# Cross-attention's key and value weights split during self-attention and kept in DRAM, and the passage between the two attentions put in another order

## What is computed

```python
x = _layernorm(tgt, ln1_g, ln1_b)
q, k, v = (_heads(t) for t in jnp.split(x @ sa_wqkv, 3, axis=-1))
wei = softmax(where(causal & ~mask, q @ k.T * scale, -inf))
result = tgt + _merge(wei @ v) @ sa_wproj + sa_bproj
xq = _layernorm(result, ln2_g, ln2_b)
xs = _layernorm(src, ln2_g, ln2_b)            # context: 750 tokens
k2, v2 = (_heads(t) for t in jnp.split(xs @ ed_wkv, 2, axis=-1))
q2 = _heads(xq @ ed_wq)
result = result + _merge(softmax(q2 @ k2.T * scale) @ v2) @ ed_wproj + ed_bproj
h = relu(_layernorm(tgt, ln3_g, ln3_b) @ ff_w1 + ff_b1)
return result + (h @ ff_w2 + ff_b2)
```

## Time and profile before

| | |
|---|---|
| median of 3 runs | 1370.09 us (1369.25 to 1372.01) |
| profiled execution, first to last instruction | 1372.2 us |
| TensorE busy | 1310.9 us, 96% |
| VectorE, GpSimd, ScalarE busy | 794.4, 701.5, 662.1 us |

### The profile page before, as it was taken

How to read it: one execution, slowest core, us unless ns; L and a number is a source line. 1 busy time by engine, 2 the same in 40 slices (tenths; PEclk the granted TensorE clock), 3 DMA queues, 4 the chain that set the end, 5 groups by cost and what they waited for, 6 DMA issues and landing times.

```text
span 1372.2 us, 24578 instructions
## 1 busy us (share of the span) xinstructions
PE 1310.9 (96%) x9193; PEld 1082.5 (79%) x9193; DVE 794.4 (58%) x2007; ACT 662.1 (48%) x1609; POOL 701.5 (51%) x577
## 2 busy tenths in 40 slices
PE   7999999999899999998788999999999999999997
PEld 6888888888788888887677787878877787887874
DVE  6613223232777777776655575756757566575565
ACT  5311111232666665666433656474665647456444
POOL 3232221322444555556733767666676766667661
PEclk9999999999999999999599999999999999999999
DMA  7400102114647776547267685777677587766641
GB/s 237 145 18 16 62 31 77 46 60 117 139 86 178 166 186 148 122 123 185 63 142 119 100 128 98 132 123 125 101 127 120 101 137 104 142 101 112 90 71 41
DMA packets 100400, 151.67 MB, mean 111 GB/s; under 512 B 10197, under 2 KB 63229, under 8 KB 99514
## 3 DMA queue, kind: packets, MB, share of 16 engines
q1 hardware_dynamic: 100282, 150.11, 53.8%
HBM read 66.74 MB, written 24.12 MB: 66 GB/s over the span
## 4 chain that ended last, share of the span: by engine, by line
PE 76%; POOL 8%; issue 5%; DVE 5%; DMA 3%; ACT 2%; SPq 1%; POOLq 0%; ACTq 0%; DVEq 0%
PE ps L1727 18%; PE ps L453 11%; PE ps L164 10%; PE ps L423 10%; PE ps_pair L1744 6%; PE ps L1759 5%; PE ps L1773 5%; PE ps L1832 3%; POOL ca_partial L1586 2%; DMA ca_k_stack<-ca_keys 2%; POOL ca_xT L1473 1%; DMA sa_K_stack<-sa_rows 1%; PE ps L1207 1%; PE ps L1791 1%; PE ps L1227 1%
## 5 line engine op out<-in xcount | busy, mean ns | idle before, releaser
L1664 DVE TENSOR_REDUCE ca_maxes<-ps 112x1 f32<-112x375 f32 x512 | 256.5, 541 | 106.0 <-PE ps L1759 103.9
L1607 ACT ACTIVATE ca_probT<-ps_pair 125x448 f32<-125x448 f32 x384 | 210.3, 554 | 181.5 <-PE ps_pair L1744 179.6
L1586 POOL TENSOR_TENSOR ca_partial<-ca_partial,ca_probT 125x896 f32<-125x896 f32 x118 | 249.2, 2112 | 93.6 <-ACT ca_probT L1607 89.0
L312 POOL TENSOR_TENSOR ff_hT<-ff_hrelu,ff_hT 128x512 fp32r<-128x512 f32 (+1 forms) x64 | 77.9, 1218 | 203.2 <-DVE ff_hT L394 203.2
L1759 PE MATMUL ps<-ca_k_stack,ca_q_stack 96*112 96x376 f32 x512 | 168.7, 352 | 6.9 <-issue 3.6
L1744 PEld LDWEIGHTS ps_pair<-ca_q_stack,ca_k_stack 98*125 98x125 f32 x768 | 130.2, 186 | 44.0 <-issue 31.9
L1744 PE MATMUL ps_pair<-ca_q_stack,ca_k_stack 98*125 98x224 f32 x768 | 156.2, 285 | 1.3 <-ACT ca_probT L1607 1.2
L423 PE MATMUL ps<-ff_w,ff_hT 128*128 128x512 f32 x672 | 155.5, 390 | 0.0
L1727 PE MATMUL ps<-w_b,ca_xT 128*125 128x512 f32 x576 | 151.2, 398 | 3.1 <-POOL ca_xT L1473 2.5
L1727 PE MATMUL ps<-ca_xT,w_a 128*128 128x376 f32 x768 | 153.1, 335 | 0.0
L423 PEld LDWEIGHTS ps<-ff_w,ff_hT 128*128 128x128 f32 x672 | 125.6, 188 | 25.8
(11 more groups left out here) (145 smaller groups left out, 2433.0 us busy)
## 6 DMA issues: line engine op xcount, KB each, us to landing
ca_k_stack<-ca_keys SPq DMA_DIRECT2D x96, 376.0 KB, 8.0
sa_Q_stack<-sa_rows SPq DMA_DIRECT2D x96, 112.0 KB, 3.5
sa_K_stack<-sa_rows SPq DMA_DIRECT2D x96, 112.0 KB, 3.7
ca_q_stack<-q_out SPq DMA_DIRECT2D x96, 112.0 KB, 9.5
ctx_tokens<-in_ctx_dram SPq DMA_DIRECT2D x14, 672.0 KB
ctx_tokens<-in_L_xattn_ff_w_dram SPq DMA_DIRECT2D x16, 512.0 KB, 4.4
q_out<-sa_yT SPq DMA_DIRECT2D x16, 448.0 KB, 3.7
wp_lo<-wp_out SPq DMA_DIRECT2D x6, 1024.0 KB, 4.8
```

Source lines behind the costliest of these rows:

```text
L312: pool.tensor_tensor(hT[:, LO, m % RING, 0:width(g)], hrelu[i % 2][:, 0:width(g)], hT[:, HI, m % RING, 0:width(g)].bitcast(F32), ALU.subtr ...
L1586: pool.tensor_tensor(total, total, half(a), ALU.add).then_inc(partial_done, 1)
L1607: act.activation(probT[u // GH][0:JT, u % GH].rearrange("p a t -> p (a t)"), ps_p[u % 2][0:JT, 0:2 * T], ACT.Exp).then_inc(exp_done, 1)
L1664: dve.tensor_reduce(maxes[:, q, j, a:a + 1], ps_s[n % 3][0:TQ, 0:JH], AX_X, ALU.max).then_inc(s_read, 1)
```

## The change

- Six units instead of two are split during batches 0 to 5 (PREPARED_WEIGHTS): the two of `ed_wproj`, two of the key half and two of the value half of `ed_wkv`. Each is loaded, rounded on ScalarE, subtracted on VectorE, and both halves go to DRAM. The key half's are written in the order of w_a's columns, which takes one more ScalarE copy for each low half (`turn_prepared`).
- In slots -17 and -16 SP loads w_a and w_b, four DMAs of 1 MB. `round_next` and `keep_next` are gone.
- The first context is loaded, measured and normalised one batch earlier: statistics in batch 6, normalises in slots 11, 13, 15 of batch 6 and 1, 3, 5 of batch 7.
- T and K of group 0 move up into slots -11 to -1; V of batch 0 to slots 5 to 8; the scores of group 0, so far in cross-attention's own slots, to slots 7 to 15; K of group 1 to slot 11. `T_rest` of the first context is on GpSimd, as it is for the others.
- The memset of ones into `k_stack` becomes an item of its own, `stack_ones`, in slot 2; some waits change with it. The statistics of context 1 go to cross-attention's own slots.

The diff, without context lines and plumbing:

```diff
@@ -581,9 +582,10 @@
-NEXT_CONTEXT = [(-2, 6), (-1, 4), (-1, 5)]
-NEXT_MEASURED = {1: (0,), 2: (1,), 7: (2,), 9: (3,), 10: (4, 5)}
-NEXT_NORMALISED = {12: (0, 1), 13: (2,), 14: (3,), 15: (4, 5)}
+NEXT_CONTEXT = [(-2, 6), (-3, 10), (-3, 11)]
+NEXT_MEASURED = {0: (2,), 1: (3,), 2: (4,), 3: (5,), 9: (0,), 10: (1,)}
+LAST_MEASURED = 1
+NEXT_NORMALISED = {11: (0,), 13: (1,), 15: (2,), 17: (3,), 19: (4,), 21: (5,)}
...
@@ -609,28 +611,32 @@
-    (-10, BEHIND): [("pad",)],
-    (-2, BEHIND): [turned(0, 0)],
-    (-1, BEFORE): [turned_rest(0, 0)],
-    (-1, BEHIND): [turned(1, 0)],
-    (0, BEFORE): [turned_rest(1, 0)],
-    (0, BEHIND): [turned(2, 0)],
-    (1, BEFORE): [turned_rest(2, 0)],
-    (1, BEHIND): [turned(3, 0)],
-    (2, BEFORE): [turned_rest(3, 0), ("context", 1, 0)],
-    (2, BEHIND): [turned(0, 1)],
-    (3, BEFORE): [turned_rest(0, 1), turned(1, 1), ("K", 0, 0, 0)],
-    (4, BEFORE): [turned_rest(1, 1), ("K", 0, 0, 1), turned(2, 1)],
-    (4, BEHIND): [("K_rest", 0, 0), turned_rest(2, 1)],
-    (5, BEHIND): [turned(3, 1), ("context", 1, 1)],
-    (6, BEFORE): [turned_rest(3, 1), ("queries", 0), *values_of(0)],
-    (7, BEFORE): keys_of(0, 1),
-    (9, BEHIND): [("K_rest", 0, 1)],
-    (11, BEHIND): values_of(1),
-    (13, BEHIND): [("statistics", 1, 0), ("statistics", 1, 1)],
-    (14, BEHIND): [("statistics", 1, 2), ("statistics", 1, 3)],
-    (15, BEHIND): [*keys_of(1, 0), ("statistics", 1, 4), ("statistics", 1, 5), ("K_rest", 1, 0), *keys_of(1, 1), ("K_rest", 1, 1),
-                   ("queries", 1), ("ones",), ("weights",)],
+    (-12, BEHIND): [("pad",)],
+    (-11, BEFORE): [turned(0, 0)],
+    (-10, BEFORE): [turned_rest(0, 0), turned(1, 0)],
+    (-9, BEFORE): [turned_rest(1, 0), turned(2, 0)],
+    (-8, BEFORE): [turned_rest(2, 0), turned(3, 0)],
+    (-7, BEFORE): [turned_rest(3, 0), turned(0, 1)],
+    (-6, BEFORE): [turned_rest(0, 1), turned(1, 1)],
+    (-6, BEHIND): [("K", 0, 0, 0)],
+    (-5, BEFORE): [turned_rest(1, 1), turned(2, 1), ("context", 1, 0)],
+    (-5, BEHIND): [("K", 0, 0, 1)],
+    (-4, BEFORE): [("K_rest", 0, 0), turned_rest(2, 1), turned(3, 1)],
+    (-3, BEFORE): [turned_rest(3, 1), ("context", 1, 1)],
+    (-2, BEFORE): keys_of(0, 1),
+    (-1, BEHIND): [("K_rest", 0, 1)],
+    (2, BEHIND): [("stack_ones",)],
+    (5, BEHIND): values_of(0),
+    (6, BEHIND): [("queries", 0), *values_of(1)],
+    (7, BEHIND): [*scores_of(0, 2), ("V", 0, 2, 0)],
+    (8, BEHIND): [*scores_of(2, 4), ("V", 0, 2, 1)],
+    (11, BEFORE): [*scores_of(4, 6), *keys_of(1, 0), ("K_rest", 1, 0)],
+    (11, BEHIND): keys_of(1, 1),
+    (12, BEFORE): [("K_rest", 1, 1), ("queries", 1), *scores_of(6, 8)],
+    (13, BEFORE): scores_of(8, 10),
+    (14, BEFORE): scores_of(10, 12),
+    (14, BEHIND): scores_of(12, 14),
+    (15, BEHIND): [*scores_of(14, 16), ("ones",), ("weights",)],
...
@@ -648,7 +654,7 @@
-    return items + [("ca",) + o for o in other[start:] if o not in early]
+    return items + [("ca",) + o for o in other if o not in early]
...
@@ -675,10 +681,11 @@
-LAST_FILLS = {0: [("Y", -2, 1)], 1: [("Y", -2, 2)], 2: [("Y", -2, 3)], 4: [("P", -1, 0)], 5: [("P", -1, 1)],
-              10: [("R", -1, 0), ("R", -1, 1)], 12: [("Y", -1, 0)], 13: [("Y", -1, 1)], 14: [("Y", -1, 2), ("Y", -1, 3)]}
+LAST_FILLS = {1: [("Y", -2, 1)], 2: [("Y", -2, 2)], 3: [("Y", -2, 3)], 4: [("P", -1, 0)], 5: [("P", -1, 1)],
+              10: [("R", -1, 0), ("R", -1, 1)], 12: [("Y", -1, 0)], 13: [("Y", -1, 1), ("Y", -1, 2)], 14: [("Y", -1, 3)]}
...
-OUTPUT_WEIGHTS = [28, 44]
+PREPARED_WEIGHTS = [12, 24, 36, 48, 60, 72]
+BY_HEADS = (2, 3)
...
@@ -699,9 +706,9 @@
-    NEXT_STATISTICS = {16 * (B - 1) + i: t for i, t in NEXT_MEASURED.items()}
-    NEXT_NORMALISE = {16 * (B - 1) + i: t for i, t in NEXT_NORMALISED.items()}
-    NEXT_WEIGHTS = [16 * (B - 1) + i for i in (-1, 0, 3, 4)]
+    NEXT_STATISTICS = {16 * (B - 2) + i: t for i, t in NEXT_MEASURED.items()}
+    NEXT_NORMALISE = {16 * (B - 2) + i: t for i, t in NEXT_NORMALISED.items()}
+    NEXT_WEIGHTS = [16 * (B - 1) + i for i in (-1, 0)]
...
@@ -759,22 +766,20 @@
-        for h in range(2):
-            if n == OUTPUT_WEIGHTS[h]:
-                items.append(("load_output", h))
-            if n == OUTPUT_WEIGHTS[h] + 8:
-                items.append(("round_output", h))
-                rests[n + 1].append(("keep_output", h))
-        if n == OUTPUT_WEIGHTS[1] + 16:
-            items.append(("stage_next",))
+        for u, first in enumerate(PREPARED_WEIGHTS):
+            if n == first:
+                items.append(("load_prepared", u))
+            if n == first + 5:
+                items.append(("round_prepared", u))
+                rests[n + 1].append(("keep_prepared", u))
+            if n == first + 9 and u in BY_HEADS:
+                items.append(("turn_prepared", u))
...
-            u = NEXT_WEIGHTS.index(n)
-            items.append(("round_next", u))
-            rests[n + 1].append(("keep_next", u))
+            items.append(("load_next", NEXT_WEIGHTS.index(n)))
...
@@ -848,11 +853,13 @@
-    ws_next = WeightSplitter(weight_halves(ed_wkv[:, 0:C], w["q"], HD) + weight_halves(ed_wkv[:, C:2 * C], w["k"]),
-                             next_stage, [sem(f"wn_landed{i}") for i in range(2)], sem("wn_hi"), sem("wn_lo"))
...
-    wo_landed, wo_hi, wo_lo, wo_stored = sem("wo_landed"), sem("wo_hi"), sem("wo_lo"), sem("wo_stored")
+    wo_landed, wo_hi, wo_lo, wo_turned, wo_stored = (sem(n) for n in ("wo_landed", "wo_hi", "wo_lo", "wo_turned", "wo_stored"))
+    next_landed = [sem(f"next_landed{i}") for i in range(2)]
+    prepared = [(source.rearrange("(k p) n -> p k n", p=P)[:, 2 * h:2 * h + 2], split[:, :, 2 * h:2 * h + 2])
+                for source, split in ((ed_wproj, wp_out), (ed_wkv[:, 0:C], kv_out[0]), (ed_wkv[:, C:2 * C], kv_out[1]))
+                for h in range(2)]
...
@@ -865,6 +872,12 @@
+    def halved(u, tile):
+        return by_heads(tile) if u in BY_HEADS else tile
+
+    def interleaved(u, tile):
+        return tile.rearrange("p k (g d j) -> p (k g) j d", g=4, d=HD) if u in BY_HEADS else tile
+
...
@@ -914,22 +927,29 @@
             ws.load(sp)
-        if name == "load_output":
-            h = item[1]
-            if h == 0:
+        if name == "load_prepared":
+            u = item[1]
+            if u == 0:
                 sp.wait_ge(ws.lo_done, 2)
             else:
-                sp.wait_ge(wo_stored, 32)
-            sp.dma_start(wo_tile, ed_wproj.rearrange("(k p) n -> p k n", p=P)[:, 2 * h:2 * h + 2]).then_inc(wo_landed, 16)
-        if name == "keep_output":
-            h = item[1]
-            sp.wait_ge(wo_hi, h + 1)
-            sp.dma_start(wp_out[HI, :, 2 * h:2 * h + 2], wo_rounded).then_inc(wo_stored, 16)
-            sp.wait_ge(wo_lo, h + 1)
-            sp.dma_start(wp_out[LO, :, 2 * h:2 * h + 2], wo_tile).then_inc(wo_stored, 16)
-        if name == "stage_next":
-            sp.wait_ge(wo_stored, 64)
-            ws_next.load(sp, 0, 2)
+                sp.wait_ge(wo_stored, 32 * u)
+            sp.dma_start(wo_tile, prepared[u][0]).then_inc(wo_landed, 16)
+        if name == "keep_prepared":
+            u = item[1]
+            sp.wait_ge(wo_hi, u + 1)
+            sp.dma_start(prepared[u][1][HI], wo_rounded).then_inc(wo_stored, 16)
+            if u not in BY_HEADS:
+                sp.wait_ge(wo_lo, u + 1)
+                sp.dma_start(prepared[u][1][LO], wo_tile).then_inc(wo_stored, 16)
+        if name == "turn_prepared":
+            u = item[1]
+            sp.wait_ge(wo_turned, BY_HEADS.index(u) + 1)
+            sp.dma_start(prepared[u][1][LO], wo_rounded).then_inc(wo_stored, 16)
+        if name == "load_next":
+            i = item[1]
+            wait_psum(sp, ("QK"[i], B - 1, KT - 1))
+            for half in (HI, LO):
+                sp.dma_start(w["qk"[i]][:, half].bitcast(F32), kv_out[i, half]).then_inc(next_landed[i], 16)
         if name == "load_columns":
...
@@ -967,14 +987,12 @@
                     .then_inc(y_stored, 16)
-        if name == "keep_next" and item[1] < 2:
-            ws_next.load(sp, item[1] + 2, item[1] + 3)
         if name == "next_context":
...
             else:
-                sp.wait_ge(ws_next.lo_done, part + 2)
+                sp.wait_ge(wo_stored, 32 * len(prepared))
             first = ctx_in[0].rearrange("(p t) c -> p t c", t=CTX_TILES)
...
@@ -1015,9 +1033,7 @@
             ln2.inverse_root(pool, item[1])
-        if name == "keep_next":
-            ws_next.keep_lo(pool, item[1])
-        if name == "next_statistics" and item[1] == CTX_TILES - 1:
+        if name == "next_statistics" and item[1] == LAST_MEASURED:
             ctx_ln.inverse_root(pool, 0)
...
@@ -1051,16 +1067,17 @@
             ws.round_hi(act, item[1])
-        if name == "round_output":
-            h = item[1]
-            act.wait_ge(wo_landed, 16 * (h + 1))
-            if h == 0:
+        if name == "round_prepared":
+            u = item[1]
+            act.wait_ge(wo_landed, 16 * (u + 1))
```

(53 more changed lines are left out.)

7 lines of the change are left out of this document (5 added, 2 removed).

## The result

The changed kernel is slower: 1374.8 us in the median of 17 runs (1373.5 to 1376.5) against 1370.7 of the kernel before (17 runs, 1369.3 to 1373.7). The ratio is 1.0027 with a 95% interval of 1.0021 to 1.0034. The forecast was 1357.4 with a range of 1347 to 1369, so the time lies outside it, and on the other side of the old time.

What follows compares the result with a forecast made beforehand. TensorE's own work bounds the kernel outside the passage from self- to cross-attention, where 31 us are waiting or half clock. Terms 0.5 + 3.2 - 1.9 + 0 - 14.5 = -12.7 us, off 1370.1: 1357.4, range 1347 to 1369.

Steps and rivals of the forecast that it cites:

- The six units: Batches 0 to 5: six prepared weight units instead of two cost 0.5 us, 4 us at worst.
- Stage 640.1 to 667.5: Output product 0 to query product 0 of batch 6: no change from 27.4 us, bounded below by 23.
- Y 0 of batch 6 to score 0 of group 1: The 63.5 us from 667.5 to 731.0 fall to 49, 14.5 less, with a new 4.8 wait at group 0's first score.
- Splitting ed_wkv leaves the last batch: Stage 622.4 to 640.1 shrinks by 1.9 us, as the 2.06 wait for a weight load goes; bounds 1.2 and 2.1.
- Batch 6: First context's inverse root and normalise 0 on GpSimd ahead of a split delay the query product by 3.2 us; bounds 0, 8.1.
- From 731 on the order is as before, so nothing is given back: From the first score of cross-attention's group 1 to the end: no change, 0 us.
- signs of being wrong: Clock of 0.50 for more than 10 us; no wait at score 0; a batch 6 longer by over 5.
- signs of being right: No weight-load wait; batch 5's query product 3 us later; longest wait at score 0; last, group 1's first score 12 earlier.
- VectorE is held by GpSimd: Rival: six normalises on GpSimd beside self-attention's copies hold VectorE, half of 13.2 us landing, 6.6: 1364 us; chance 0.10.
- The clock stays down: Rival: clock stays at 0.50 from thin slots -8 to -6 past score 0, +21 us, 1378 us; chance 0.12.

Runs made afterwards that it cites:

- the second profile of before: The kernel before, with nothing changed, profiled once more: a span of 1371.8 us and a time of 1373.9 us.
- all mends together: Changed kernel with units 1 and 2 moved, memset at slot 4, query stack 1 early, normalises and low halves on VectorE, bias addition later: 1359.8 us, 0.9909.

## Why the prediction was wrong

*The six units* failed as a step. It said that such a unit lies beside products, 0.5 us in all and 4 at worst. Its price came from a batch whose unit has one cast and no second. It counted casts, subtractions and transfers as work and did not follow the new wait: the second cast needs a store to have landed, and the store's place in SP's queue is behind a stack that waits for GpSimd. Measured +5.3 by batch 6; moving units 1 and 2 (6.0 back) and the one cast (5.3 back) showed it.

*Stage 640.1 to 667.5, "I take no change"*, failed as well: +6.2 (+5.3 against the second profile of before). The step named the queue (the low half behind inverse root and finish) and then priced it at nothing; its own bound went only downwards. Separate runs, whose shares may overlap, put some 2 us on the half clock and 2.5 on the low halves on GpSimd with what it held of VectorE (33.6 to 31.0); all mends together give 4.3 (29.3). Each of these is uncertain by about 1, as the stretch takes 32.4 to 33.8 where nothing in it was changed. The last 1.9 above the old 27.4 were not taken apart; the stretch has 22.7 us of products for TensorE now, where it had 15.0.

*Y 0 of batch 6 to score 0 of group 1* was right: 50.6 us for 49, with the new wait at its place and of its size. *Splitting ed_wkv leaves the last batch* was right, 2.0 for 1.9. *Batch 6* was right in size (2.9 for 3.2), in part by luck: 0.7 of it arose in slots 4 to 6, where the prediction saw nothing, and 2.2 at the place it named. Of these the normalises were 0.7 in two runs and nothing in a third; that the inverse root is the rest is not shown.

*"From 731 on the order is as before, so nothing is given back"* was off by 2.1 (1.0 against the second profile): behind the wait of 3.58 two half products of the keys took 2.08 and 2.07 us, at half clock, where those of before took 1.20 (second row).

```profile
730.94 2.08 PE L1747 MATMUL ps<-ca_xT,w_a 128*128 128x376 f32 x6
...
731.23 1.20 PE L1727 MATMUL ps<-ca_xT,w_a 128*128 128x376 f32 x6
```

None of the signs of being wrong appeared. Of the signs of being right the last failed: the first score of group 1 came 0.5 us earlier in the span, not 12.

Of the rivals, *VectorE is held by GpSimd* had the mechanism, and put it in the wrong place: not the normalises in batch 6, but finish, low halves and bias addition behind output product 1, and the memset as soon as it was moved. (The 2.85 us that the prediction sets beside its rule on copies is a subtraction with two inputs in SBUF.) The Trainium skill (SBUF — State Buffer, Who interferes with whom) has it as an exclusive hold of a shared port pair by whichever engine issues first, for its whole instruction; it excepts VectorE's instructions with a single SBUF input outside the two-port modes. The rows agree: 4.46 and 5.65 beside the memset, and 0.69 for the statistics in the same 10 us. *The clock stays down* was part of the loss, at some 2 us where it had 21.

Two readings of the prediction are off, and no term of its sum hangs on them: TensorE's busy dent is in slices 18 to 21, counted from 0, which is 617 to 755 us and not 652 to 789; and by its own 27.4 and 22.7 the stage of 640 to 667 has 4.7 us to spare in the rival of the clock, not 6.

## What to carry to other kernels

Work that fits beside the bound engine is free only where its waits are free too: for each wait that an edit adds, follow the thing waited for back through every queue it stands in, to the first engine that is late. An item moved on GpSimd has two prices, what queues behind it there and what VectorE does beside it; look for a place where VectorE reads PSUM or has nothing to do. And before a reordering is thrown out for being slower, its steps are worth pricing one by one: here a handful of collisions hid a gain of 0.9%.

## What the runs showed of the hardware

A VectorE instruction held by GpSimd lasts to the end of GpSimd's instruction, whatever its own size: 112x2 elements took 4.46 us. Which ones are held depends on both: beside the memset, which only writes, scalar operations were held (4.46; 5.65 for two), the statistics (0.69) and a subtraction of two SBUF inputs (0.39) were not; beside the bias addition, which reads, such a subtraction took 1.58 instead of 0.62. GpSimd is held in turn: half a split took 2.34 instead of 0.67 beside a subtraction of VectorE. Casting a weight unit into the order by heads costs ScalarE 2.06 us instead of 1.03, and VectorE's subtraction 2.00 instead of 1.21 where neither is held. And granted clock is a poor measure of loss in a stretch where other engines set the pace: bringing it from 0.8 to 1.00 over 32 us gave back some 2 us there.
